# First attention heads: the values product issued one key tile later, between the two pairs of scores, and both maxima products at the end of the tile

## What is computed

```python
def _L0_attn_ref(x, Wq, Wk, Wv, Wff, bff):
    NUM_HEADS = 16
    ...
    q = x @ Wq.T * (1.0 / jnp.sqrt(jnp.asarray(D, x.dtype)))
    k = x @ Wk.T
    v = x @ Wv.T
    ...
    scores = jnp.einsum('bqhd,bkhd->bhqk', q, k)
    attn = jax.nn.softmax(scores, axis=-1)
    out = jnp.einsum('bhqk,bkhd->bqhd', attn, v).reshape(B, S, D)
    return out @ Wff.T + bff
```

## Time and profile before

| | us |
|---|---|
| median of 3 runs | 4393.2 (4388.37 to 4426.04) |
| the profiled execution, its own time | 4392.84 |
| its span, first to last instruction | 4391.3 |
| second pass of the first heads within it | 577 to 1976, 1399.0 |
| PE, DVE, ACT busy over the span | 3866.8, 2943.7, 2287.0 |
| mean granted TensorE clock over the span | 0.918 |

### The profile page before, as it was taken

One profiled execution on the slowest core, in us unless ns is written; L12 is line 12 of the kernel. 1 busy time (PEld: TensorE's weight loads), 2 busy tenths in 40 slices (PEclk: granted clock), 3 DMA queues, 4 the chain that ended last, 5 costly groups with the idle time before them and its releaser, 6 DMA issues. The chain is left out here.

```text
span 4391.3 us, 74529 instructions
## 1 busy us (share of the span) xinstructions
PE 3866.8 (88%) x23584; PEld 2207.0 (50%) x23584; DVE 2943.7 (67%) x5544; ACT 2287.0 (52%) x4361; POOL 821.5 (19%) x904
## 2 busy tenths in 40 slices
PE   7796689999999999995889796479999999996799
PEld 5685433333333333323778455346566566663455
DVE  7676688888888888836766536456666566662433
ACT  2353257777777777760245122135556566564322
POOL 5345200000000000001543414412212122120000
PEclk8898789999999999977999898779989899998799
DMA  5464713232323233103355204767666667652400
GB/s 88 98 200 154 197 17 49 33 49 33 48 33 48 38 44 45 22 6 110 37 168 174 76 18 127 197 180 191 181 172 183 167 183 188 176 145 65 128 26 29
DMA packets 217648, 452.77 MB, mean 103 GB/s; under 512 B 57018, under 2 KB 129722, under 8 KB 200506
## 3 DMA queue, kind: packets, MB, share of 16 engines
q1 hardware_dynamic: 180026, 358.80, 34.7%
q0 software_dynamic: 37248, 89.24, 7.5%
HBM read 272.59 MB, written 182.63 MB: 104 GB/s over the span
## 5 line engine op out<-in xcount | busy, mean ns | idle before, releaser
L1769 DVE TENSOR_REDUCE full_tops<-psum 128x1 f32<-128x1024 f32 x1024 | 1206.4, 1219 | 168.2 <-PE psum L1677 168.1
L1730 ACT ACTIVATE full_probs<-psum 128x512 f32<-128x512 f32 x2048 | 1066.1, 603 | 305.3 <-PE psum L1649 305.1
L2238 ACT ACTIVATE causal_probs<-psum 128x512 f32<-128x512 f32 (+3 forms) x1280 | 640.3, 533 | 404.7 <-PE psum L2110 232.7
L1649 PE MATMUL psum<-full_q,full_k 49*128 49x512 f32 x2048 | 658.5, 479 | 20.3 <-ACT full_probs L1730 13.7
L2289 DVE TENSOR_REDUCE causal_tops<-psum 128x1 f32<-128x1024 f32 (+7 forms) x704 | 586.9, 858 | 116.1 <-PE psum L2161 116.0
L1649 PEld LDWEIGHTS psum<-full_q,full_k 49*128 49x128 f32 x2048 | 287.3, 188 | 608.3 <-ACT full_probs L1730 571.4
L1658 PE MATMUL psum<-full_probs,full_vh 128*32 128x512 f32 x4096 | 562.0, 621 | 0.7 <-ACT full_probs L1730 0.7
L1677 PE MATMUL psum<-full_k,full_q 48*128 48x512 f32 x2048 | 402.7, 457 | 51.2 <-DVE full_negident L1762 23.5
L2110 PE MATMUL psum<-causal_q,causal_k 49*128 49x512 f32 (+3 forms) x1280 | 410.5, 454 | 12.5 <-ACT causal_probs L2238 8.3
L2161 PE MATMUL psum<-causal_k,causal_q 48*128 48x512 f32 (+4 forms) x1152 | 327.9, 416 | 68.9 <-DVE causal_tops L2304 32.6
L2140 PE MATMUL psum<-causal_probs,causal_vh 128*32 128x384 f32 (+3 forms) x3712 | 346.3, 436 | 1.2 <-ACT causal_probs L2238 1.2
(11 more groups left out here) (252 smaller groups left out, 5723.1 us busy)
## 6 DMA issues: line engine op xcount, KB each, us to landing
causal_bias<-bias_tiles SPq DMA_DIRECT2D x32, 1280.0 KB, 6.4
band_scores<-xn POOLq DMA_DIRECT2D x256, 160.0 KB, 4.4
moe_w_raw<-in_moe_w SPq DMA_DIRECT2D x44, 768.0 KB, 5.6
full_q<-qk_split SPq DMA_DIRECT2D x192, 128.0 KB, 5.6
full_k<-qk_split SPq DMA_DIRECT2D x192, 128.0 KB, 6.8
causal_q<-rot_parts SPq DMA_DIRECT2D x192, 128.0 KB, 5.3
causal_k<-rot_parts SPq DMA_DIRECT2D x192, 128.0 KB, 6.4
slot_outputs<-moe_y SPq DMA_DIRECT2D x42, 512.0 KB, 3.2
```

The source lines that it names most:

```text
L1649: nc.tensor.matmul(k.psum[:, b, :], k_sb[at, q, kt * P:(kt + 1) * P], q_sb[at, q, n * BLK:(n + 1) * BLK], start=True, stop=True).then_inc( ...
L1730: nc.scalar.activation(pT[:, kt % 4, n * BLK:(n + 1) * BLK], k.psum[:, bank(q, u), :], ACT.Exp).then_inc(p_ready, 1)
L1769: nc.vector.reduce_max(mx[:, q % 2, u // 2, u % 2:u % 2 + 1], src, AX_X).then_inc(m_free, 1)
L2238: nc.scalar.activation(dst, k.psum[:, bank(q, u), 0:(hi - lo) * P], ACT.Exp).then_inc(p_ready, 1)
```

## The change

PE's order for a tile becomes: S3 of kt, S0 of kt+1, W of kt-1, S1 and S2 of kt+1, two maxima products, and (at tile 11) `row` behind them. W of tile 15 moves into tile 0 of the next head, and the last one stands behind the last head. ACT's copy `out` of head i-1 therefore moves from the end of head i-1 into tile 1 of head i, between E1 and E2. Since the first head has no W before it, PE and ACT run it apart, ahead of the hardware loop, and their loop rounds start at heads 1, 9 and 17; DVE and POOL keep the old loop, with rounds at heads 0, 8 and 16. No instruction of the engines is added or taken away.

```diff
+def full_heads_loop_late(eng, first, body):
+
+    first()
+    with eng.Fori(0, NH // 8 - 1) as it:
+        for x in range(1, 9):
+            body(it * 8 + x, x % 4, 2)
+    for x in range(1, 8):
+        body(NH - 8 + x, x % 4, min(7 - x, 2))
...
-                def body(i, q, left):
+                def body(i, q, left, first=False):
                     ring = segment(q, left)
                     for kt in range(KT):
-                        score(i, q, kt, 3)
+                        former = (i, q, kt - 1) if kt > 0 else (i - 1, (q + 3) % 4, KT - 1)
                         after = (i, q, kt + 1) if kt + 1 < KT else (i + 1, (q + 1) % 4, 0)
                         more = kt + 1 < KT or left
+                        score(i, q, kt, 3)
                         if more:
                             score(*after, 0)
-                        for ahead, h, p in ring[2 * kt:2 * kt + 2]:
-                            far(i + ahead, h, p)
+                        if kt > 0 or not first:
+                            weighted(*former)
                         if more:
                             score(*after, 1)
                             score(*after, 2)
-                        weighted(i, q, kt)
+                        for ahead, h, p in ring[2 * kt:2 * kt + 2]:
+                            far(i + ahead, h, p)
                         if left and kt == ROW_KT:
                             row(i + 1, (q + 1) % 4)
 
-                full_heads_loop(pe, body)
+                full_heads_loop_late(pe, lambda: body(0, 0, 2, True), body)
+                weighted(NH - 1, (NH - 1) % 4, KT - 1)
...
-                def body(i, q, left):
+                def body(i, q, left, first=False):
                     exps(i, q, 0, (3,))
                     for kt in range(1, KT):
-                        exps(i, q, kt, range(NQ))
+                        if kt == 1 and not first:
+                            exps(i, q, kt, (0, 1))
+                            out(i - 1, (q + 1) % 2)
+                            exps(i, q, kt, (2, 3))
+                        else:
+                            exps(i, q, kt, range(NQ))
...
-                    out(i, q % 2)
-
-                full_heads_loop(act, body)
+
+                full_heads_loop_late(act, lambda: body(0, 0, 2, True), body)
+                out(NH - 1, (NH - 1) % 2)
```

## The result

Over 20 runs each the changed kernel takes 4443.09 us (4405.14 to 4464.87), the kernel before 4404.25 (4385.1 to 4429.0). The ratio is 1.008, with a 95% interval of 1.0061 to 1.0099: slower by about 35 us (27 to 44), four fifths of a per cent. The forecast was 4409 with a range of 4380 to 4450, so 16 us over the profiled execution of before.

The account below looks back on a forecast made before the run. Waits, not a full engine, bound the kernel: a loop of latencies of 2.60 us a tile. +22.5 at `row` and -6.5 at the copy made +16 on 4392.8, so 4409; forecast 4400 to 4430, wider range 4380 to 4450.

Parts of the forecast that it names:

- Part 1: The ordinary tile: the new order makes the same loop with other names, 2.60 us again, so a change of 0.
- the loop: Latencies that pace an ordinary tile: score S1, exponential E1, the S0 wanting its bank, W, next S1; 2.60 us a round.
- Rival B: W's weights load while S0 is in flight, 0.11 behind its load, not 0.43: -91 to -115 us, 4294 to 4318; chance 0.13.
- Part 2: At `row`, PE waits for DVE's `top`: 1.35 instead of 0.60 us, +0.75 in 30 heads, +22.5 us (21 to 32).
- the sum: The forecast's total for the kernel: +22.5 for `row` and -6.5 for the copy, +16 on 4392.8, 4409.
- Part 3: ACT's copy `out`, now between exponentials: 0.04 instead of 0.25 us, -0.21 in 31 heads, -6.5 us (-7 to 0).
- Rival A: The clock falls at `row`, costing 1.5 to 4.4 us more, 30 times: +44 to +132, 4453 to 4541; chance 0.13.
- Part 4: The rest, SP's queue and the loop jumps of PE and DVE: 0 to +6 us, taken as 0.

Follow-up runs that it names:

- experiment 5: The changed kernel with both maxima products put back between the pair S3, S0 and W: 5299.98 against 4499.98 for the kernel before.
- experiment 6: The changed kernel with `row` moved behind W of tile 12 and one of the two maxima products put between S0 and W: 4806.71, a single run.
- experiment 9: The changed kernel with `row` behind W of tile 12, half of W and one product in each gap, one start flag: ratio 0.9868 to the kernel before.
- experiment 1: The changed kernel with `row` alone moved, behind W in tile 12: 4481.7 against 4499.98 for the kernel before, ratio 0.9957.
- experiment 2: The kernel before with `row` alone moved, directly behind the maxima products and ahead of S1, S2 and W: 4445.59 against 4397.65, ratio 1.0104.
- Experiment 3: The kernel before with only PE's and ACT's loop rounds changed to start at heads 1, 9 and 17: 4492.41 against 4499.98, ratio 0.9985.
- experiment 7: The changed kernel with `row` behind W of tile 12 and W cut into two halves, both in W's place: ratio 0.9981 to the kernel before.
- experiment 8: The changed kernel with `row` behind W of tile 12, half of W and one product in each gap: ratio 0.9857 to the kernel before.

## Why the prediction was right, point by point

**Part 1, the ordinary tile: right.** 2.60 was forecast and 2.61 measured, and experiments 5, 6 and 9 show the loop by making it longer and shorter. Rival B is out: in the 512 tiles of the changed kernel W's weights never load less than 0.42 behind the load of the score ahead of them (0.42 to 0.44 in 446 of them, more at a clock of 0.50 or after the copy), although W's semaphore is satisfied long before. By the Trainium skill ("TensorE: Matmul & The Clock Gate", "Step-by-step: what each phase is for") a weight load can go ahead of matmuls in flight where row groups don't conflict or the background buffer is its target; for these loads over all 128 rows, behind a score on part of them, no trace here shows it. Beneath W itself weights over all 128 rows do load: those of `row` in experiment 1 at 704.53, while W runs from 704.00 to 705.07.

**Part 2, `row`: right.** 1.35 forecast, 1.28 measured. The wait had the place, the releaser and the followers that the prediction gave it, and experiments 1 and 2 take it away and bring it back with this one move. Against the 0.60 of before this is +0.68 a head for the +0.75 of the sum.

**Part 3, the copy: right in sign, too large.** -0.21 a head was forecast. Measured is 0.14 - 0.25 = -0.11: W's load comes 0.12 after the end of the copy, not 0.05 (630.72 after 630.60), and the next score follows it by 1.02 instead of 0.99.

**Left out.** The first S0 of a head waits for the row's DMA as well as for its bank. Before, this S0 was off the loop; S2 was the critical score. Now S0 is critical: its load comes 0.17 after the end of E1 (668.21 after 668.04) instead of 0.05, and that tile takes 2.72: +0.11. That it is this second wait and its instructions is my reading of the place; no run takes them away. The three errors together make about +0.7 a head instead of +0.54, some 21 us instead of 16.

**Rival A came true in part, on top of the forecast.** It was given 0.13 and priced apart, as a fall in nearly every head that costs 1.5 to 4.4, at least 44 us in all. It came in 11 of 30 heads in one profile and 6 in the other, at 1.2 to 2.3 each, which makes 17 us in the first. The argument against it, that the clock stays at 1.00 from 1905 to 1920 without any product, was too weak: there PE never stands still for 1.06 us at a stretch (0.55 at most). The 21 us of the tiles alone lie outside the 27 to 44 of the result; with the falls they fit.

**The number.** The direction and the tiles were forecast, but the measured +35 is over twice the forecast +16. The median of 4443 lies 34 over the 4409: 11 of them because before has a median of 4404 over 20 runs and the forecast started from one execution of 4393, 5 because of its own sum, and the other 17 are, as far as the profile shows, the falls of the clock, which the sum put at nothing. The range held it with 7 us to spare. That is partly luck: a fall in most heads, at the same price, would have left it.

**Part 4: right.** Experiment 3 shows that the loop's rounds cost nothing.

## What to carry to other kernels

When engines are paced by a loop through a few banks, moving work within the tile renames the loop and doesn't shorten it; write the loop down (matmul, consumer, the matmul that wants its bank, all that PE does up to the next turn) and ask which pieces lie in it. In the ordinary tile only less work between two turns helped: half a W instead of a whole one in each gap, at no cost for the cut. And of a group of work that is moved, look last at the small rare instruction behind it: `row` stands once in sixteen tiles, and losing its cover cost more than everything else in the change.

## What the runs showed of the hardware

- Behind a stretch of 1.06 us in which PE had no matmul, once in 43 us, the granted clock fell to 0.50 in some heads and not in others: in 11 of 30 in one profile, 6 in the next, 8 with the same wait in the kernel before, and none where the wait was taken away. What decides it from head to head is open.
- A low clock can last. With two products in the loop the tile is 3.09 at 1.00 and 4.92 at 0.50, and the clock stayed at 0.50 from 1745 to 2833 us. In the kernel before, with a tile of 4.07 at 0.50, it was back after 13.7 us at most at the two loop jumps; it stayed low for long only at the start of the pass and in the last head. That the longer tile itself keeps the clock low fits this, but no run shows it by itself.
- Four matmuls side by side in 32 columns each cost the same as eight of half the length: 1.00 us from W's load to the next score's, whole or cut (experiment 7).
- A start (the flag that opens a sum) on one half of a bank spoils the sum that the other half has begun in the same 32 partitions: with it the sums of experiments 7 and 8 are wrong, without it experiment 9 has the whole sum. This agrees with the Trainium skill ("PSUM — Partial Sum Buffer", "The four PSUM rules"), by which the first matmul of a group clears the marks of the whole bank.
